# Moving 64 transposing DMAs from ScalarE's queue to SyncE's, in a fused AdaLN-FFN kernel on one core

## What is computed

```python
w = weights[conditions]                              # 64 of 200 matrices of 64x64
y = einsum('bct,bcd->bdt', x, w)                     # x is 64 x 64 x 512
h = hbitlinear(y, w_up, 8)                           # 4096 tokens, 512 -> 1024
h = square(relu(h))
return x + hbitlinear(h, w_down, 8)                  # 1024 -> 512, and the residual

def hbitlinear(x, w, bits):
    xq = act_quant(fwht(x), bits)                    # Walsh-Hadamard, then 8 bits a token by its largest value
    wq = weight_quant(w)                             # ternary, scaled by the mean of abs(w)
    return einsum('bsd,fd->bsf', xq, wq)
```

## Time and profile before

| | us |
|---|---|
| median of 3 runs | 308.59 |
| lowest and highest run | 307.69, 308.90 |
| span of the profiled execution | 308.8 |
| a tile in the steady part (residual to residual) | 16.1 to 16.2 |
| busy: PE, DVE, ACT, POOL | 254.4, 272.1, 184.3, 171.9 |

### The profile page before, as it was taken

One profiled execution on the slowest core, in us unless ns is written; L12 is line 12 of the kernel. 1 busy time (PEld: TensorE's weight loads), 2 busy tenths in 40 slices (PEclk: granted clock), 3 DMA queues, 4 the chain that ended last, 5 costly groups with the idle time before them and its releaser, 6 DMA issues.

```text
span 308.8 us, 6571 instructions
## 1 busy us (share of the span) xinstructions
PE 254.4 (82%) x1864; PEld 208.0 (67%) x1864; DVE 272.1 (88%) x410; ACT 184.3 (60%) x237; POOL 171.9 (56%) x200
## 2 busy tenths in 40 slices
PE   0376898869799989798998989898989898786773
PEld 0375787859587868686877868687877667564441
DVE  1269999999999999999999999999999998977660
ACT  1077677678584857566656676767575757643310
POOL 8033334859476676767565657574747466364600
PEclk9999999999999999999999999999999999988996
DMA  6675611235597453543444242333343434223262
GB/s 205 226 305 171 174 30 35 89 99 129 130 162 164 88 159 90 141 106 126 103 145 89 86 85 85 68 102 60 93 83 93 91 97 102 70 68 88 82 151 87
DMA packets 67049, 35.16 MB, mean 114 GB/s; under 512 B 57170, under 2 KB 57170, under 8 KB 67026
## 3 DMA queue, kind: packets, MB, share of 16 engines
q10 hardware_dynamic: 51200, 12.59, 22.4%
q1 hardware_dynamic: 15826, 22.29, 21.5%
HBM read 13.89 MB, written 8.39 MB: 72 GB/s over the span
## 4 chain that ended last, share of the span: by engine, by line
DVE 39%; issue 27%; POOL 12%; PE 7%; ACT 4%; DMA 3%; ACTq 3%; DVEq 2%; SPq 1%; POOLq 1%
DVE u_max L722 7%; DVE g L708 7%; DVE g L702 5%; PE u_ps L585 5%; POOL x_half L341 4%; DVE out_sb L753 4%; DVE zq L741 4%; DVE y_lo L678 3%; DVE uq L747 2%; DVE z_max L683 2%; ACTq L473 2%; DMA x_all<-in_L_ffn_w_up_dram 2%; POOL u_deq L382 2%; DVE u_abs L729 2%; POOL z_kept L348 2%
## 5 line engine op out<-in xcount | busy, mean ns | idle before, releaser
L374 POOL TENSOR_TENSOR p_lo<-g,p_hi 128x1024 fp32r<-128x1024 f32 x32 | 76.1, 2397 | 58.9 <-ACT p_hi L453 54.9
L585 PE MATMUL u_ps<-had_r,p_hi 128*128 128x256 f32 x256 | 66.4, 295 | 26.4 <-ACT u_rint L461 26.4
L585 PEld LDWEIGHTS u_ps<-had_r,p_hi 128*128 128x128 f32 x256 | 50.4, 197 | 32.1 <-issue 32.1
L570 PE MATMUL h_ps<-zqT,w_upT 128*128 128x256 bf16 x512 | 66.6, 273 | 0.7 <-issue 0.3
L585 PE MATMUL u_ps<-had_r,p_lo 128*128 128x256 f32 x256 | 64.9, 289 | 0.0
L595 PE MATMUL o_ps<-w_downT,uqT 128*128 128x512 bf16 x256 | 62.2, 387 | 3.2 <-DMA uqT<-uq 2.4
L702 DVE TENSOR_TENSOR g<-g 128x1024 f32<-128x1024 f32 x32 | 61.7, 1937 | 0.0
L341 POOL TENSOR_TENSOR x_half<-x_all 128x512 f32<-128x512 f32 (+1 forms) x32 | 45.9, 1438 | 21.3 <-DMA x_all<-in_x_dram 15.5
L440 ACT ACTIVATE g<-h_ps 128x512 f32<-128x512 f32 x64 | 36.5, 600 | 32.9 <-issue 21.6
L570 PEld LDWEIGHTS h_ps<-zqT,w_upT 128*128 128x128 bf16 x512 | 47.6, 98 | 8.5 <-issue 1.2
L537 PE MATMUL y_ps<-w_diag,x_half 128*128 128x128 f32 (+1 forms) x256 | 37.3, 292 | 18.4 <-DMA w_diag<-in_L_cond_weights_dram 11.9
(11 more groups left out here) (44 smaller groups left out, 310.6 us busy)
## 6 DMA issues: line engine op xcount, KB each, us to landing
x_all<-in_x_dram SPq DMA_DIRECT2D x16, 512.0 KB, 3.8
out_dram<-out_sb SPq DMA_DIRECT2D x32, 256.0 KB, 2.0
x_all<-in_L_ffn_w_up_dram SPq DMA_DIRECT2D x2, 1024.0 KB, 6.9
x_all<-in_L_ffn_w_down_dram SPq DMA_DIRECT2D x2, 1024.0 KB, 6.0
w_diag<-in_L_cond_weights_dram SPq DMA_DIRECT2D x64, 16.0 KB, 2.4
zqT<-zq ACTq DMA_TRANSPOSE x32, 2.4
uqT<-uq ACTq DMA_TRANSPOSE x32, 3.1
x_all<-in_hadamard_dram SPq DMA_DIRECT2D x1, 256.0 KB, 3.7
```

Source lines behind the costliest of these rows:

```text
L374: nc.gpsimd.tensor_tensor(p_lo[par][:, :, i], g[par][:, :, i], p_hi[par][:, :, i].bitcast(FP32), ALU.subtract).then_inc(s_plo[k], 1)
L570: mm = nc.tensor.matmul(h_ps[u % 2][:, i, :], w_upT[:, q, f * P:(f + 1) * P], zqT[par][:, q, :], start=(q == 0), stop=(q == TC - 1))
L585: mm = nc.tensor.matmul(u_ps[:, blk * 256:(blk + 1) * 256], part[par][:, 2 * blk + i, k * P:(k + 1) * P], had_r[:, i, :], start=(i == 0 an ...
```

## The change

The 64 transposing DMAs leave ACT's list and are issued by SP. SP's program is written out in steps of its own. In step s it goes through the list below and waits in each place until that item's inputs are ready. x and the gathers of tile s + 2 are issued in step s, so two tiles ahead. All addresses in SP's program are now constants but the row of the gathered matrix. A semaphore that only counted the transposes (s_turn) is gone. No other engine's program changes.

```diff
-SPLIT = W_PAIRS // (2 * KP)
-AHEAD = SPLIT + 2
+RAW_FREE = W_PAIRS // KP
...
+            def load_x(t):
+                if t >= 2:
+                    sp.wait_ge(s_x[t % 2], XLOADED * (t // 2))
+                if t >= RAW_FREE:
+                    sp.wait_ge(s_hr, 1)
+                    sp.wait_ge(s_wturn[0], 4)
+                    sp.wait_ge(s_wturn[1], 4)
+                sp.dma_start(x_all[:, t * KP:(t + 1) * KP, :],
+                             x_v[:, t * KP:(t + 1) * KP, :]).then_inc(s_x[t % 2], XLOADED)
+
+            def gather_w(t, j):
+                if j == 0 and t >= 2:
+                    sp.wait_ge(s_wc[t % 2], LOADED * (t // 2))
                 sp.wait_ge(s_zero, 1)
                 sp.wait_ge(s_cond, 16)
+                pair = t * KP + j
+                for two in range(2):
+                    row = sp.value_load(cond_sb[0:1, 2 * pair + two:2 * pair + two + 1],
                                         min_val=0, max_val=S_SETS - 1)
...
+            def turn_z(t, k):
+                for u in range(4):
+                    after(sp, s_h[u], t - 1)
+                sp.wait_ge(s_zq[k], t + 1)
+                sp.dma_start(zqT[t % 2][:, :, k * P:(k + 1) * P], zq[k][:, :], transpose=True)\
+                    .then_inc(s_zqT[k], 16)
+
+            def turn_u(t, k):
+                after(sp, s_o[k], t - 1)
+                sp.wait_ge(s_uq[k], t + 1)
+                sp.dma_start(uqT[t % 2][k][:, :, :], uq[k][:, :], transpose=True).then_inc(s_uqT[k], 16)
+
+            def store(t, k):
+                sp.wait_ge(s_out[k], t + 1)
+                sp.wait_ge(s_zero, 1)
...
+            for s in range(TILES + 8):
+                def at(lag, s=s):
+                    return 0 <= s - lag < TILES
+
+                if at(2):
+                    turn_z(s - 2, 1)
+                if at(-2):
+                    load_x(s + 2)
+                if at(6):
+                    turn_u(s - 6, 1)
+                if at(-2):
+                    gather_w(s + 2, 0)
+                if at(5):
+                    turn_u(s - 5, 0)
+                if at(-2):
+                    gather_w(s + 2, 1)
+                if at(7):
+                    store(s - 7, 0)
+                if at(1):
+                    turn_z(s - 1, 0)
+                if at(7):
+                    store(s - 7, 1)
...
-            def turn_z(t, half, par, k):
-
-                for u in range(4):
-                    after(act, s_h[u], t - 1)
-                act.wait_ge(s_zq[k], t + 1)
-                act.sem_inc(s_turn, 1)
-                act.dma_start(zqT[par][:, :, k * P:(k + 1) * P], zq[k][:, :], transpose=True)\
-                    .then_inc(s_zqT[k], 16)
...
                 run(square, 3, 0)
-                run(turn_z, 2, 1)
                 run(relu, 3, 2)
...
                 run(quant_u, 5, 0)
-                run(turn_u, 6, 1)
                 run(y_high, 0, 1)
...
                 run(square, 3, 1)
-                run(turn_u, 5, 0)
...
                 run(p_high, 4, 1)
-                run(turn_z, 1, 0)
```

More of the change, by code:

```diff
@@ L167, in ffn_kernel @@
         s_wT = sems("wT_ready", 2)
-        s_turn = sem("turn_may_start")
         s_xh = sems("x_half_ready", 2)
@@ L247, in _ @@
             sp.dma_start(cond_sb[:, :], cond.rearrange("(o b) -> o b", o=1)).then_inc(s_cond, 16)
[L249 to L264, removed]
+            def load_x(t):
[10 more added lines that the diff above has]
+                    sp.wait_ge(s_wc[t % 2], LOADED * (t // 2))
                 sp.wait_ge(s_zero, 1)
                 sp.wait_ge(s_cond, 16)
-                for n in range(2 * KP):
-                    row = sp.value_load(cond_sb[0:1, bass.ds(2 * pair + n, 1)],
+                pair = t * KP + j
+                for two in range(2):
+                    row = sp.value_load(cond_sb[0:1, 2 * pair + two:2 * pair + two + 1],
                                         min_val=0, max_val=S_SETS - 1)
-                    lo = C * (n % 2)
+                    lo = C * two
                     sp.dma_start(
-                        w_diag[lo:lo + C, bass.ds(pair + n // 2, 1), lo:lo + C],
+                        w_diag[lo:lo + C, pair:pair + 1, lo:lo + C],
                         w_cond[bass.ds(row, 1), :, :].rearrange("s c d -> c s d"),
-                    ).then_inc(s_wc[par], 16)
+                    ).then_inc(s_wc[t % 2], 16)
             def load_weight(n, h):
@@ L280, in load_weight @@
                              view[:, h * rows:(h + 1) * rows, :]).then_inc(s_wraw[n][h], 16)
[L282 to L292, removed]
+            def turn_z(t, k):
[11 more added lines that the diff above has]
+                sp.wait_ge(s_zero, 1)
+                sp.dma_start(out_v[:, KP * t + k:KP * t + k + 1, :],
+                             out_sb[k][:, :].rearrange("p (o t) -> p o t", o=1)).then_inc(s_store[k], 16)
+            load_x(0)
             sp.dma_start(had_f, had).then_inc(s_had, 16)
@@ L295, in _ @@
             gather_w(0, 0)
+            gather_w(0, 1)
             load_weight(0, 1)
-            load_x(0, 1)
-            gather_w(0, 1)
+            load_x(1)
+            gather_w(1, 0)
+            gather_w(1, 1)
             load_weight(1, 0)
             load_weight(1, 1)
[L301 to L321, removed]
+            for s in range(TILES + 8):
[19 more added lines that the diff above has]
+                    store(s - 7, 1)
             for k in range(KP):
@@ L467, in cast_u_act @@
                 nc.scalar.activation(uq[k][:, :], u_rint[:, :], ACT.Copy, bias=-RINT).then_inc(s_uq[k], 1)
[L469 to L473, removed]
             def step(run, once):
```

## The result

The changed kernel takes 328.53 us (median of 4 runs, 327.53 to 329.31); the kernel before, run beside it, takes 308.75 us (4 runs, 307.69 to 309.87). The ratio is 1.0624, with the interval 1.058 to 1.0669. The forecast was 321.5 us, with a range up to 328. So it is slower, as forecast, but by 6.2% and not by 4%. The profiled execution of after is the one at 329.31 us; its span is 327.5 us, 18.7 above the span of before. A ratio goes by the executions of one batch on one chip and leaves out those in a slower state of the chip, so it can differ a little from the ratio of the two medians.

What follows compares the result with a forecast made beforehand. The prediction took DVE's full instruction list to bound the steady tiles. It summed 308.8 + 12.4 (seven tiles) + 0.4 (the end) + 0 = 321.6, said 321.5 us, with a range of 314 to 328.

Steps and rivals of the forecast that it cites:

- closed chain: Cast of uq (k = 0), transpose issue, two gathers, store, landing, residual (k = 0): 6.24 us after the cast, before 3.25.
- How many tiles: Tiles with both gathers and stores in SP's steps: 7 tiles (residuals of tiles 1 to 7), 7 x 1.77 = 12.4 us.
- two gathers 2.62: Chain term on SP between the transpose's issue and the store: 1.35 + 1.27 us.
- from the store's issue to the residual 2.18: Chain term from SP's store issue to DVE's next residual, read where DVE stood waiting for that landing: 2.18 us.
- give-back of the held g_outer: DVE's g_outer, held until POOL's p_lo ends, becomes short once the residual is late: gives 1.1 to 1.5 us back.
- just in time: SP's store of k = 1 goes out at about +5.75 us and lets DVE on at about +7.9.
- bandwidth shared in proportion: Alternative to the lock between POOL and DVE: less comes back, a tile grows by up to 2.99 us, sum 330.1.
- C: Rival: uq (k = 1) transposes wait behind slow x loads, residual some 1 us late in 7 to 9 tiles; 329, 8%.
- B: Rival: the held g_outer absorbs the whole wait, leaving only 0.4 us at the end; 309.2 us, 7%.
- ACT's relief at nothing: 78.7 us of issue time leave ACT's queue, but DVE's full list covers it: 0 taken.
- The shared queue: Transposes on SP's queue beside x, gathers and stores: landing times unproven by any run, other moved things put at 0.
- The bound upward: Gathers at the loop's pace and landings held up by transposes on the same queue, up to 0.9 us a tile: 327.9.

Runs made afterwards that it cites:

- stores_first: Changed kernel with both stores of tile s-7 at the head of SP's step, ahead of all transposes and gathers: 308.72 us, ratio 0.9992.
- in_place: Changed kernel with the residual written over x in x_all and stored from there, so no residual waits for a store: 308.83 us, ratio 0.9969.
- loads_ahead: Changed kernel with only the second gather pair's two register loads moved ahead of the transpose of uq (k = 0): 320.53 us, ratio 1.036.
- four_gathers: Changed kernel with all four gathers of a tile between the transpose of uq (k = 0) and the store: 347.81 us, ratio 1.1265.
- residuals_together: stores_first with the residual of k = 1 moved ahead of the first g_outer in DVE's step: 302.26 us, ratio 0.9795.
- store_behind_turn: Changed kernel with the store of k = 0 directly behind the transpose of uq (k = 0), the second gather pair after it: 329.11 us, ratio 1.0677.
- both_behind_turn: Changed kernel with both stores directly behind the transpose of uq (k = 0), gathers and transpose of zq after them: 311.97 us, ratio 1.0086.

## Why the prediction was right in kind and short in size

**The mechanism: right.** The closed chain is there, with the landing as the releaser of each residual of k = 0 in tiles 1 to 7, and it vanishes with either of its two conditions (stores_first, in_place).

**How many tiles: right.** The growth is in seven tiles. Behind them the chain is 3.8 to 4.1 us against 3.62 forecast, and from tile 7 to the end the kernel loses 0.5 us, against 0.4.

**The chain: forecast 6.24 us, measured 6.97.** In the tile shown it is 6.86, and term by term: cast to the end of the transpose's issue 1.34, as forecast (0.09 + 1.25). From there to the store's issue 218.02 - 214.91 = 3.11 us, where two gathers and the waits were put at 2.62 + 0.10. From the store's issue to the residual 2.41, where 2.18 was taken. The failed step is *the price of what stands directly behind a transpose or another DMA*, in the terms "two gathers 2.62" and "from the store's issue to the residual 2.18". The gathers were priced from the earlier trace rows, where the first follows an x load and the others each other. Behind this transpose the first register load takes 0.73 us and not 0.28 as there: + 0.45. The store was priced from the earlier trace rows, where it goes out alone after a long wait: 0.33. Directly behind another DMA its issue takes 0.53: + 0.20. Together 0.65, where 0.62 us were missed in this tile. The mean is 0.11 longer than this tile: in tile 3 the store went out 0.35 us later, and in tiles 1, 4 and 6 the residual came 2.5 to 2.6 us after it. The traces of loads_ahead and four_gathers bear the prices out, a register load ahead of the transpose at 0.27 and a further gather at 1.24, though the time of loads_ahead missed its forecast.

**The give-back of the held g_outer: right, 0.1 us less than taken.** g_outer fell to 1.20 us; r1 - r0 (from the residual of k = 0 to that of k = 1) is 1.97 where 0.73 + 1.13 = 1.86 was forecast, since the store of k = 1, "just in time", is 0.1 us late. (It was put at +5.75 with DVE going on at +7.9; its own terms, 4.06 + 1.21 + 0.4, give +5.67. Measured are +6.49 and +8.93.) The Trainium skill's lock (SBUF — State Buffer, "Who interferes with whom") fits the runs of both kinds: the time came back in full when DVE started the instruction later, and residuals_together turned it into a gain. The forecast of 330.1 us for a bandwidth shared in proportion lies nearer to the measured time than 321.5, but r1 - r0 fell by 1.27 us, so it is not what happened.

**The sum.** The k = 1 residual stands at 6.97 + 1.97 = 8.94 us after the cast, forecast 8.10: 0.84 us a tile. Another 0.11 is in the rest of the tile (2.71 against 8.94 - 6.34 = 2.60). That is the wait for POOL's z_kept shown above, which the prediction did not have: the stretch from the residual of k = 1 to the next cast takes 9.92 to 9.98 us in the six tiles with it, 9.85 in the one without it, and 9.79 to 9.88 before. In sum 0.95 us a tile was missed, 0.73 of it in the chain. 321.6 + 7 x 0.95 - 0.6 (tile 0 is early) + 0.1 (the end) = 327.7, against the span of 327.5.

**The rivals.** C, transposes that suffer behind x, had forecast 329, which is nearer to the measured time than 321.5. It is not what happened: the transposes of uq land after 3.1 us as before, DVE stands before its residuals for stores (37.9 us) and for PE's o_ps only once (1.6 us), and stores_first has the same transposes behind the same x loads at 308.72 us. B failed too: the wait is not absorbed.

**ACT's relief at nothing: right.** ACT no longer waits on its own issuing, 21.6 us in all before. stores_first gives it this relief without the loss: there ACT stands in front of z_col for 51.2 us instead of 32.9, and the time gains nothing (0.9992). After, it is 66.3 us, part of which is only the longer kernel.

**The shared queue: priced at nothing, and right.** The landings of the transposes are 2.4 and 3.1 us on either queue, and stores_first is as fast as before. The Trainium skill (DMA: Bandwidth & Descriptors, "Issuing engines are not separate DMA queues") says that DMAs of all issuing engines run on the same DMA engines, and these rows agree. It also says that issuing from several engines saves only the sequencer's time; here the measurement decides otherwise, since 18.7 us came from what stands in front of what in one list that is worked off in order.

**The bound upward** (0.9 us a tile for slow gathers and landings) was nearly the right size, 0.95 being needed. It was put at the far end. The cause is that every price had been read at a place where the instruction did not follow a transpose, and no row of before showed it in such a place on SP.

## What to carry to other kernels

Before putting a DMA into another engine's list, write down for each item behind it when it is ready and who waits for it; a store with a single buffer should not stand behind a transfer whose input is made late. Moving the stores to the head of the step, or giving them no buffer to free, cost nothing here, and both are small edits. Price an issue by a row where it follows the same kind of neighbour. And when a DVE instruction is twice as long as its twin, look at which of its neighbours in the list could take its place: that one line gave 2% with the transposes on either queue.

## What the runs showed of the hardware that was not expected

- A register load from SBUF on SP takes 0.26 to 0.28 us behind an x load or a gather, and about 0.5 right behind a store (0.48 in store_behind_turn, 0.52 in both_behind_turn). After, it takes 0.73 right behind the transpose of uq (k = 0) and 0.96 behind that of k = 1 in the same tile. A store's issue takes 0.33 us alone and 0.53 right behind another DMA.
- PE was granted less clock in the kernels in which it waited more, though not in every tile with the same waits. The stretches of three tiles after (columns as in the earlier trace rows; the column behind POOL's is the granted clock):

```profile
145.10:163.98 18.88, 16.32 (x112) 13.81 (x112) 14.59 (x25) 10.58 (x14) 10.29 (x12) 0.91 0.39 102
163.98:182.68 18.70, 15.02 (x112) 12.37 (x112) 14.54 (x25) 10.44 (x14) 10.36 (x12) 1.00 0.40 101
182.68:201.68 19.00, 16.32 (x112) 13.84 (x112) 14.53 (x25) 10.66 (x14) 10.36 (x12) 0.91 0.40 102
```

Before, seven tiles of the same part all had 1.00, with PE busy 14.6 to 15.1 of 15.9 to 16.7 us. After, four of six had 0.91, which lies between the two levels of 2.4 and 1.2 GHz, with PE's busy time 1.3 us longer for the same 112 matmuls. No share of this can be seen in the length of a tile: the shortest of the six, 18.65 us, has 0.91. Over the profiled executions the clock is 0.936 in four_gathers, with the longest waits, 0.950 after, 0.980 before and 0.989 in stores_first. The other executions of after had 0.963 to 0.974, so this one shows the effect at its largest.
